# Attention in a two-layer kernel: row tiles of 64 rows, exponentials over one and two banks in turns, operands loaded a stage earlier

## The reference, cut to what matters

```python
qkv = x @ W_attn + b_attn
q, k, v = (split_heads(t) for t in jnp.split(qkv, 3, axis=-1))   # [B=4, H=16, T=1024, D=8]
q, k = apply_p_rope(q, positions, D), apply_p_rope(k, positions, D)
attn = jnp.einsum('bhqd,bhkd->bhqk', q, k) / scale
attn = jnp.where(causal_mask, attn, jnp.finfo(attn.dtype).min)
attn = jax.nn.softmax(attn, axis=-1)
y = jnp.einsum('bhqk,bhkd->bhqd', attn, v)
return y.transpose(0, 2, 1, 3).reshape(B, T, C) @ W_proj + b_proj
```

## Time and profile before

| what | us |
|---|---|
| median of 3 runs | 1701.14 (1697.91 to 1708.54) |
| the profiled execution | 1688.48 |
| its span in the trace | 1687.1 |
| attention, from the table load to the last output | 139.56 to 717.1 |
| VectorE busy over the span | 937.2 (56%) |
| TensorE matmul busy over the span | 1117.3 (66%) |
| ScalarE busy over the span | 622.7 (37%) |

### The profile page before, as it was taken

How to read it: one execution, slowest core, us unless ns; L and a number is a source line. 1 busy time by engine, 2 the same in 40 slices (tenths; PEclk the granted TensorE clock), 3 DMA queues, 4 the chain that set the end, 5 groups by cost and what they waited for, 6 DMA issues and landing times. The chain is left out here.

```text
span 1687.1 us, 22339 instructions
## 1 busy us (share of the span) xinstructions
PE 1117.3 (66%) x7477; PEld 697.6 (41%) x7477; DVE 937.2 (56%) x1993; ACT 622.7 (37%) x1394; POOL 473.4 (28%) x486
## 2 busy tenths in 40 slices
PE   4472598999899899855529799304727550099991
PEld 4231233433333343244315687204625440077771
DVE  6684676776677677287002444498772850044444
ACT  1251266666666666633103344122201120044440
POOL 2236011111111111101760355313600027533441
PEclk9776799999999999965759899657858655599996
DMA  4622111111111111002110222300236041112215
GB/s 122 256 91 84 45 38 44 53 51 45 47 55 50 41 52 44 1 1 66 51 49 1 54 77 75 102 22 0 102 92 193 19 116 51 48 46 56 58 51 159
DMA packets 106320, 110.10 MB, mean 65 GB/s; under 512 B 15057, under 2 KB 94052, under 8 KB 102756
## 3 DMA queue, kind: packets, MB, share of 16 engines
q1 hardware_dynamic: 76388, 80.21, 15.7%
q0 software_dynamic: 8704, 17.97, 3.2%
q10 hardware_dynamic: 21120, 10.49, 2.2%
HBM read 65.88 MB, written 38.26 MB: 62 GB/s over the span
## 5 line engine op out<-in xcount | busy, mean ns | idle before, releaser
L762 DVE TENSOR_REDUCE part<-sps 128x1 f32<-128x640 f32 (+6 forms) x352 | 346.4, 1026 | 146.8 <-PE sps L617 143.7
L728 ACT ACTIVATE prob<-tps 128x512 f32<-128x512 f32 (+1 forms) x640 | 316.2, 558 | 240.5 <-PE tps L674 235.5
L1372 POOL DMA_INDIRECT yk<-yo,place x144 | 143.5, 997 | 241.5 <-ACT yo L1394 234.8
L524 POOL TENSOR_SCALAR_AFFINE_SELECT prob<-prob 128x512 f32<-128x512 f32 x128 | 80.0, 637 | 467.4 <-ACT prob L728 467.4
L1405 DVE TENSOR_TENSOR ehid<-esg,epg 128x176 f32<-128x176 f32 (+1 forms) x144 | 61.9, 430 | 266.8 <-ACT esg L1386 241.1
L1452 PE MATMUL epg<-up,xT 128*128 x576 | 162.7, 407 | 4.8 <-issue 2.4
L651 PE MATMUL ops<-prob,vs 128*32 128x512 f32 (+3 forms) x1536 | 156.8, 496 | 5.1 <-POOL prob L524 5.1
L1290 POOL DMA_INDIRECT xg<-h,slot x128 | 123.8, 967 | 38.9 <-issue 38.0
L614 PE MATMUL sps<-operands 128*128 128x512 bf16 (+3 forms) x384 | 98.7, 334 | 45.1 <-DMA operands<-qk 30.0
L674 PE MATMUL tps<-operands 128*128 128x512 bf16 (+3 forms) x384 | 100.4, 329 | 22.4 <-DMA operands<-mrow 11.4
L1471 PE MATMUL epd<-down,ehidT 128*128 (+1 forms) x720 | 107.8, 280 | 7.4 <-ACT yo L1394 5.4
(11 more groups left out here) (315 smaller groups left out, 1842.5 us busy)
## 6 DMA issues: line engine op xcount, KB each, us to landing
xg<-empty SPq DMA_DIRECT2D x2, 4680.0 KB, 18.0
xt<-xg SPq DMA_DIRECT2D x144, 65.0 KB, 1.8
gat<-yk ACTq DMA_DIRECT2D x32, 256.0 KB, 4.6
tz<-kpad SPq DMA_DIRECT2D x8, 1024.0 KB, 7.2
qk<-term SPq DMA_DIRECT2D x24, 256.0 KB, 2.1
operands<-qk SPq DMA_DIRECT2D x32, 192.0 KB
odd_operands<-qk SPq DMA_DIRECT2D x32, 192.0 KB
wr<-powr SPq DMA_DIRECT2D x8, 516.0 KB, 3.2
```

The costliest lines, as they stand in the source:

```text
L524: nc.gpsimd.affine_select(out=blk, in_=blk, pattern=[[0, HQ], [1, P]], compare_op=ALU.is_ge, fill=0.0, base=0, channel_multiplier=-1).then ...
L728: nc.scalar.activation(prob[c % 2][:, h, 0:n], tps[:, k % 3, 0:n], ACT.Exp, scale=float(HD) ** -0.5).then_inc(exp_done, 1)
L762: freed(nc.vector.tensor_reduce(part[p][:, heads[0]:heads[-1] + 1, i:i + 1].rearrange("p h o -> p (h o)"), src, AX.X, ALU.max, negate=True))
L1372: nc.gpsimd.indirect_dma_start(out=d.yk, out_offset=bass.IndirectOffsetOnAxis(ap=place[:, u:u + 1], axis=0), in_=yo[u][:], in_offset=None) ...
```

## The change

**Row tiles.** The operands of a quad are one buffer `qk[t % 4]` of [128, 2, 2, 1024]: partitions 0 to 49 hold heads x = 0, 1 of side s = 0, partitions 64 to 113 those of side s = 1; index 0 is q, 1 is k. Both passes read the same buffer. A matmul names `tile_position=(64 * s, 0)`, so it uses 64 of the array's 128 rows. `s_item` makes items of at most two banks, bank s for side s; there are 20 of them, each over at most 512 keys; for keys from 512 on the maxima go to `part2`, and one `min` joins them with `part`. The mask's 128x128 product becomes two of 64 rows, `half`, a full one and one of 64 columns, for each head.

**Exponentials.** The 40 units (chunk, head) of a quad are taken as items of one, two, one, two ... units: a single one uses `tpb` (one bank), a double one `tpa` (two banks) and one exponential over both. Chunk widths are 512, 384, 384, 4 x 512, 384, 384, 512, so both banks of an item have one width. `prob` has four buffers (`PBUF`).

**Order.** `place_of` gives each of the 20 x 16 first-pass items a slot among the 27 of each quad, up to 1.3 quads ahead; `values` stands three or four items behind the last exponential of its chunk. Before the first slot stand quad 0's items, three of quad 1 and quad 0's maxima.

**Loads.** `load_quad` makes 12 DMAs a quad, six for each side (before, six for each of the two sets); quads 0 to 3 are loaded from SP's queue in the projection stage, between the stores of its steps 2 to 5. The rows of ones come by DMA. The memsets of the operand buffers are gone, in both stages.

The core of the diff (the blocks of the other helpers follow the same pattern):

```diff
+                def first_loads(b, u):
+                    if b == 1 and u == 0:
+                        for half in range(2):
+                            sp.wait_ge(stored[half], 16 * 3)
+                    if b > 0 and 2 * b + u < 6:
+                        load_quad(sp, w, d, 2 * b + u - 2)
+                staged(sp, NS, (0, store), (0, first_loads))
...
+UNITS = [(0, 0), (1, 0), (0, 1), (1, 1)]
+PBUF = [0, 1, 2, 3, 0, 1, 2, 0, 1, 3]
+def _items():
+    out, units = [], [(c, u) for c in range(NCH) for u in range(HQ)]
+    while units:
+        n = 1 + len(out) % 2
+        out.append(units[:n])
+        units = units[n:]
+    return out
...
+SITEMS = []
+for _i in range(TPB):
+    for _c0 in range(0, (_i + 1) * P, ST):
+        _n = min(ST, (_i + 1) * P - _c0)
+        SITEMS += [(_i, _c0, _n, [0, 1])] if _n <= ST // 2 else [(_i, _c0, _n, [0]), (_i, _c0, _n, [1])]
...
+def place_of(t, n):
+    k = NS * t + n
+    return int(max(1.35 * k - 36, 1.08 * (k - 23)) // 1)
...
+        sps = [ps(f"sps{p}", [P, 2, ST]) for p in range(2)]
+        tpa, tpb = ps("tpa", [P, 2, ST]), ps("tpb", [P, 1, ST])
...
+                def max_to_rows(t):
+                    sp.wait_ge(s_free, MAX_AT[t])
+                    for s in range(2):
+                        for r in range(2):
+                            at = 64 * s + KR + r
+                            sp.dma_start(qk[t % 4][at:at + 1, 0].rearrange("o x (k q) -> o (x k) q", k=TPB),
+                                         mrow[t % 2][16 * s:16 * s + 16, r, :]).then_inc(m_in[t % 4], 16)
...
+                def s_item(t, n):
+                    i, c0, wd, heads = SITEMS[n]
+                    if n == 0:
+                        pe.wait_ge(qk_in[t % 4], LOADED * (t // 4 + 1))
+                    out = acquire()
+                    diag = c0 + wd == (i + 1) * P
+                    for at, x in enumerate(heads):
+                        for s in range(2):
+                            lo = 64 * s
+                            ins = nc.tensor.matmul(out[:, s, at * wd:(at + 1) * wd], qk[t % 4][lo:lo + KR, 0, x, i * P:(i + 1) * P],
+                                                   qk[t % 4][lo:lo + KR, 1, x, c0:c0 + wd], start=True, stop=not diag,
+                                                   skip_group_check=True, tile_position=(lo, 0))
+                        for u in range(2 * diag):
+                            for s in range(2):
+                                lo = 64 * s
+                                ins = nc.tensor.matmul(out[:, s, (at + 1) * wd - P + 64 * u:(at + 1) * wd], w.half[lo:lo + 64, 0, u, :],
+                                                       w.half[lo:lo + 64, 1, u, 64 * u:], start=False, stop=u == 1,
+                                                       skip_group_check=True, tile_position=(lo, 0))
+                    filled(ins)
...
+                for t in range(NQUAD):
+                    for m, units in enumerate(TITEMS):
+                        act.wait_ge(t_ready, NTI * t + m + 1)
+                        at = PBUF[c] * HQ + u
+                        nc.scalar.activation(prob[:, at:at + len(units), 0:n], slot_of(t, m)[:, :, 0:n], ACT.Exp,
+                                             scale=float(HD) ** -0.5).then_inc(exp_done, 1)
```

More of the change, by code:

```diff
@@ new lines, with load_quad @@
+BEFORE, RING = _ring()
+MAX_AT = {}
+_n = 0
+for _it in BEFORE + [it for t in range(NQUAD + 1) for m in range(NTI) for it in RING[t, m]]:
+    _n += 1
+    if _it[0] == MAXT:
+        MAX_AT[_it[1]] = _n
+PAIR = 2 * T
+def load_quad(sp, w, d, t):
+    b, quad, buf = t // NQ, t % NQ, w.qk[t % 4]
+    row = 0
+    for n, rows in enumerate((3, 2, 1)):
+        for side, term, step in ((0, n, 0), (1, 0, C * T)):
+            for s in range(2):
+                at = b * (3 * C * T) + quad * (HD * HQ * T) + (side * NB * 3 + term) * (C * T) + s * PAIR
+                src = bass.AP(d.qk.tensor, at, [[step, rows], [HQ * T, HD], [1, PAIR]])
+                lo = 64 * s + row * HD
+                sp.dma_start(buf[lo:lo + rows * HD, side].rearrange("p x t -> p (x t)"), src).then_inc(w.qk_in[t % 4], 16)
+        row += rows
@@ L588, in _ @@
+                max_to_rows(0)
+                for t in range(NQUAD):
+                    if t + 1 < NQUAD:
+                        max_to_rows(t + 1)
+                    if t + 4 < NQUAD:
+                        sp.wait_ge(t_ready, NTI * (t + 1))
+                        load_quad(sp, w, d, t + 4)
             @block.tensor
             def _(pe):
-                item = [0, 0]
-                def slot():
-                    return sps[(item[1] + par[0]) % 2]
-                par = [0]
+                used = [0]
@@ L597, in acquire @@
                 def acquire():
-                    n = item[0] + item[1]
-                    if not (isinstance(n, int) and n < 2):
-                        pe.wait_ge(s_free, n - 1)
+                    after(pe, s_free, used[0] - 1)
+                    return sps[used[0] % 2]
                 def filled(ins):
                     ins.then_inc(s_ready, 1)
-                    item[1] += 1
-                def s_item(n, p):
-                    i, heads, step = SITEMS[n]
-                    acquire()
-                    out = slot()
-                    for x, h in enumerate(heads):
-                        for c0 in range(0, (i + 1) * P, ST):
-                            n1 = min(ST, (i + 1) * P - c0)
-                            diag = c0 + n1 == (i + 1) * P
-                            ins = nc.tensor.matmul(out[:, x * step + c0:x * step + c0 + n1], qa[p][:, h, i * P:(i + 1) * P],
-                                                   ka[p][:, h, c0:c0 + n1], start=True, stop=not diag, skip_group_check=True)
-                        e = x * step + i * P
-                        ins = nc.tensor.matmul(out[:, e:e + P], w.identb[:], w.maskb[:], start=False, stop=True, skip_group_check=True)
-                    filled(ins)
@@ new lines, in values, with after_item @@
+                    ins.then_inc(pv_done, 1)
+                def after_item(t, m):
+                    for c in range(NCH):
+                        at = NTI * t + m - LAST[c] - (4 if c in OPENING else 3)
+                        if at % NTI == 0 and 0 <= at // NTI < NQUAD:
+                            values(at // NTI, c)
+                    ring(RING[t, m])
+                ring(BEFORE)
+                pe.wait_ge(w.ones_in, 8 * 16)
+                for t in range(NQUAD):
+                    pe.wait_ge(m_in[t % 4], ROWS * (t // 4 + 1))
+                    for m in range(NTI):
+                        scores(t, m)
+                        after_item(t, m)
@@ L804, in project_phase @@
+                for t in range(NQUAD + 1):
+                    for m in range(NTI):
+                        ring(RING[t, m])
 def project_phase(nc, w, d):
```

418 lines of the change are left out of this document (165 added, 253 removed).

## The result

The changed kernel takes **1590.85 us** (median of 4 runs, 1585.61 to 1598.09) against 1699.53 (4 runs, 1695.87 to 1708.54): ratio 0.9356, 95% interval 0.9303 to 0.9409. Forecast: 1580, range 1540 to 1645. The profiled execution is the slowest of the four, 1598.09 us, so its stages are set against the 1688.48 of before with that in mind: 90.4 us less there, 108.7 between the medians.

What follows compares the result with a forecast made beforehand. Attention was taken as bound by TensorE's 28.4 of 33.0 us a quad plus waits. Opening to 169.0 plus 427 us body ends attention at 596 instead of 717.1, 121 us less: 1580 us, range 1540 to 1645.

Steps and rivals of the forecast that it cites:

- Row tiles: TensorE's two score passes: two row tiles run at the same time, first pass 7.7 to 3.85 us, transposed pass 5.2.
- the prediction's estimate: Score passes at the skill's packing efficiency, 3.07 for four tiles: about 2 us more a quad, some 30 us above forecast.
- the factor: Waits in turns on top of TensorE's work a quad: 1.16, carried over from before, making 23.3 us into 27.0.
- the rival of tiles in turns: Row tiles do not overlap: TensorE 30.9 us, 35.8 us a quad with waits, 1709 us in all; chance 0.05.
- VectorE alone the bound: Rival for the quad's period: TensorE always has a bank ready, VectorE sets 24.5 us a quad, 1543 us; chance 0.23.
- just enough: Transposed-score slots: the two-bank slot refills (0.38 us a matmul) during the 0.5 us single exponential; value chunks of 1.1 us stop ScalarE.
- Worth nothing by itself: Exponentials over two banks, 27 instead of 40 a quad: save 0.8 us on ScalarE, which waits anyway.
- Cover is there, so I count 0, and up to 4 us: SP's 48 added loads in the projection stage: hidden, cost 0, up to 4 us if the queue delays the last store.
- The sign of the loss: Listed sign of a wrong forecast: stores of the projection stage that land after 139.6.
- Opening: Attention's start to first transposed scores: from 139.6 to 169.0 instead of 192.03, saving 23.0 us.
- TensorE at 1.00 through the stage: Sign that the forecast is right: TensorE's granted clock stays at 1.00 throughout attention.
- Body: Attention after its opening: 14.6 quads at 27.0 us, 394, plus 29.5 and 3.5 for the tail, 427 us.

Runs made afterwards that it cites:

- one_side: Changed kernel with both heads of a pair on the same 64-row tile, in both passes and the masks; ratio 1.168 to the kernel before, 56.6 us a quad.
- one_bank_exp: Changed kernel with one exponential issued per bank, 40 a quad instead of 27; ratio 0.935 to the kernel before, 26.44 us a quad.
- two_early: Changed kernel with only quads 0 and 1 loaded in the projection stage, quads 2 and 3 at attention's start; ratio 0.923 to the kernel before.
- spread: Like the changed kernel, but six loads in each of four projection steps, two quads loaded at attention's start; ratio 0.926 to the kernel before.
- three_banks: The six-loads-a-step kernel with transposed scores through three one-bank slots, 40 exponentials a quad; ratio 0.933 to the kernel before, 27.61 us a quad.

## Why the prediction was right, and where it was not

**Row tiles.** Right. Two tiles together: 18 pairs of 0.23 = 4.1 us for the first pass (3.85 counted), 11.5 x 0.23 + 13 x 0.213 = 5.4 for the second (5.2). Masks 16 x 0.08 = 1.3, where I took 2.4 between 1.3 and 3.5: the low end, where only streaming counts. A pair of tiles gave 1.85 times one (2 x 0.213 / 0.23), so of the 2 us a quad in the prediction's estimate 0.5 came (4.1 + 5.4 against 3.85 + 5.2). With values, transposes and the 0.6 for changes of shape (not measured apart) 22.6 instead of 23.3, and 26.31 / 22.6 = 1.16. That the factor held is partly luck: I had carried it over without a reason of its own, and in `one_side` at full clock it was not 1.16 but 31.85 / 30.9 = 1.03, so the rival of tiles in turns was priced too high at 35.8.

**"VectorE alone the bound" (24.5).** Near, but not it: halving VectorE's work still leaves 25.57. What is left, about 25 us, is TensorE's work and the slots that I described under ScalarE as "just enough", in shares that no run separates. The rule of the Trainium skill named with this rival, TensorEngine Tiling (Array Packing), section PSUM Bottleneck, holds so far as the reduces take 341.8 us as they took 346.4; that VectorE then bounds the quad alone, the runs deny.

**"Worth nothing by itself"**, of the exponentials over two banks. Near enough: `one_bank_exp` puts it at 0.13 us a quad.

**"Cover is there, so I count 0, and up to 4 us"**, for SP's 48 loads: this step failed. The stage took 17.1 us more from its first store on. I had counted SP's time to issue (right for the first step, 8.8 us), but not that stores behind 12 loads take up to 12.0 us to land, nor that ScalarE waits for the stores. With the loads spread thinner the stage took 65.3 us again. The sign of the loss stood in the list of what would show the forecast wrong; its price was 4 us at most.

**The memset of GpSimd**, counted among the things that simply go: it held VectorE and with it the whole stage. Its absence brings the first store 5.4 us earlier, in the other direction; the net of the two is the 11.7 of the table.

**Opening.** 28.4 against 29.4 counted, right. The queue ahead of the rows is gone: they land within 3.5 us. The sign "TensorE at 1.00 through the stage" did not come true here: from 151 to 180 us the granted clock was 0.50.

**Body.** 433.5 against 427. The last cast came 393.6 us after the first transposed scores, 394 counted, which is luck: two errors cancel, 26.3 instead of 27.0 us a quad and 15.0 of these periods (393.6 / 26.31), not 14.6. The tail from there took 40.0, not 33: the clock, which I had seen at 0.99 in the last quad of before, fell. TensorE's timeline in the last quad, the chunk of values of 512 columns:

```profile
580.77 1.83 PE L704 MATMUL ops<-prob,vs 128*32 128x512 f32 x8
```

1.83 us instead of 1.06. The tail's length goes with the clock granted over it, from the last cast to the last output: 40.0 us at a mean of 0.79 here and in `two_early`, 37.7 at 0.86 in `spread`, 33.9 at 1.00 in `three_banks`, whose order is another. Why the clock fell there, and whether fewer rows at work is the cause, no run tried.

In sum 11.7 - 1.0 + 6.5 = 17.2 us later than forecast at the end of attention, and the median came 10.9 above it. That the median missed by less is no merit of the sum: the forecast carried 12.7 us over from the profiled execution of before to the median, while this one is 7.2 above its own, and 13.5 lie behind attention (17.2 + 13.5 - 12.7 - 7.2 = 10.8).

**The fastest.** `two_early` and `spread`, 0.923 and 0.926, beat both kernels; against `one_bank_exp`, in the changed kernel's place, their ratios are 1.3 and 1.0% less, without overlap of the intervals. Between the two, the times tell nothing.

## What to carry to other kernels

An early load is free only if neither its issue nor its transfer stands ahead of a store that someone waits for: put few per step, and look for the store's time to landing, not only the queue's. When a bound engine gets faster by 5 us a quad, take away each remaining engine's work in turn before you name the next bound: here 9 us of VectorE's work gave 0.7 us a quad, the masks' 1.3 us gave 0.8, and the rest lies between TensorE and ScalarE. And read the granted clock beside the busy time: with one row tile at a time TensorE was marked always busy and ran at 0.50, so the second tile was worth 56.6 to 26.3 us a quad in most quads and not the 31.85 to 26.3 of the streaming alone. The kernel before, with its rows filled up by zeros, had no such loss to win back.

## What the runs showed of the hardware that was not expected

- Granted clock 0.50 with TensorE marked busy 40.00 of 40 us, with matmuls of 48 to 50 rows one at a time, with or without a tile position; 1.00 with two such tiles side by side.
- Two row tiles of 512 columns 0.23 us, one 0.21; four mask matmuls (two of 128, two of 64 columns) in two tiles 0.08 us.
- A 0.33 us instruction of VectorE took 6.96 us, the length of the memset that GpSimd ran at the time.
- Twelve loads took SP 7.22 us to issue in the first step that had loads and 9.81 in the fourth, and a store behind them up to 12.0 us to land instead of 2.1; behind six loads a step at most 5.1, behind the same bytes in 24 loads 3.3.
